# A transformer block on one core: in the lead-in to attention, the placements of the queries go ahead of the swaps on SyncE's queue

## The reference, cut to what matters

```python
# x: (2, 1024, 512); 32 query heads, 8 key/value heads, head size 64
h = _layernorm(x) * (1 + ca) + sa
q = (h @ Wq).reshape(b, s, H, D).transpose(0, 2, 1, 3)
k = (h @ Wk).reshape(b, s, KVH, D).transpose(0, 2, 1, 3)
v = (h @ Wv).reshape(b, s, KVH, D).transpose(0, 2, 1, 3)
q, k = apply_rope(q, pos), apply_rope(k, pos)      # [t1*cos - t2*sin, t1*sin + t2*cos]
scores = einsum('bhqd,bhkd->bhqk', q, repeat(k, 4)) / sqrt(64)
attn = softmax(where(causal, scores, min))
x = x + ga * (einsum('bhqk,bhkd->bhqd', attn, repeat(v, 4)) @ Wo)
h = _layernorm(x) * (1 + cb) + sb
x = x + gb * ffn(h)          # ternary weights, silu gate, rms norm
```

## Time and profile before

| | |
|---|---|
| runs | 1933.04, 1933.71, 1939.78 us; median 1933.71 |
| profiled execution | 1939.95 us, span 1938.1 us, so 1.9 us lie around the span |
| TensorE busy | 1772.3 us, 91% of the span, mean granted clock 0.97 |
| VectorE, ScalarE, GpSimd busy | 1269.1, 1144.7 and 964.6 us |
| attention's first matmul | at 68.7 us |
| first scores of the lead-in | at 111.8 us |
| first transposes of group 0 (L682) | at 127.0 us |

### The profile page before, as it was taken

How to read it: one execution, slowest core, us unless ns; L and a number is a source line. 1 busy time by engine, 2 the same in 40 slices (tenths; PEclk the granted TensorE clock), 3 DMA queues, 4 the chain that set the end, 5 groups by cost and what they waited for, 6 DMA issues and landing times. The chain is left out here.

```text
span 1938.1 us, 28246 instructions
## 1 busy us (share of the span) xinstructions
PE 1772.3 (91%) x9585; PEld 1423.4 (73%) x9585; DVE 1269.1 (65%) x2079; ACT 1144.7 (59%) x2307; POOL 964.6 (50%) x773
## 2 busy tenths in 40 slices
PE   8579999999999999999999999985999599999997
PEld 7367777777777778778777777764888478787876
DVE  6358788778888788788777878783233345444443
ACT  3257777777777877778777777783223243323221
POOL 0127576666666666666765666651000044444443
PEclk8789999999999999999999999997999799999999
DMA  7034353344344343344444433426555200101000
GB/s 258 12 93 114 85 135 108 90 129 110 88 126 109 94 124 101 109 115 108 117 106 102 120 98 91 129 77 225 174 174 176 95 1 1 50 1 50 1 28 22
DMA packets 174922, 190.97 MB, mean 99 GB/s; under 512 B 31408, under 2 KB 117688, under 8 KB 174784
## 3 DMA queue, kind: packets, MB, share of 16 engines
q1 hardware_dynamic: 137792, 140.99, 25.5%
q10 hardware_dynamic: 36992, 48.25, 8.9%
HBM read 86.12 MB, written 31.74 MB: 61 GB/s over the span
## 5 line engine op out<-in xcount | busy, mean ns | idle before, releaser
L814 DVE TENSOR_TENSOR p_lo<-ps_b,p_hi 128x512 fp32r<-128x512 f32 x576 | 395.5, 687 | 193.1 <-ACT p_hi L740 189.0
L753 ACT ACTIVATE p<-ps_b,negm 128x640 f32<-128x640 f32 (+7 forms) x512 | 381.5, 748 | 114.0 <-DVE negm L822 111.3
L740 ACT CAST p_hi<-ps_b 128x512 fp32r<-128x512 f32 x576 | 336.8, 588 | 158.3 <-PE ps_b L682 155.5
L822 DVE TENSOR_REDUCE negm<-ps_b 128x1 f32<-128x640 f32 (+7 forms) x512 | 376.3, 745 | 40.0 <-PE ps_b L674 39.3
L682 PE MATMUL ps_b<-ident,p 128*128 128x128 f32 x2304 | 350.0, 274 | 3.2 <-DVE p_lo L814 2.1
L672 PE MATMUL ps_b<-k_hh,q_hl 128*128 128x512 f32 (+3 forms) x768 | 272.5, 355 | 39.2 <-ACT p L753 36.2
L694 PE MATMUL ps_b<-p_hi,v_hl 128*128 128x512 f32 x576 | 276.7, 480 | 16.3 <-ACT o_sb L746 16.0
L682 PEld LDWEIGHTS ps_b<-ident,p 128*128 128x128 f32 x2304 | 258.7, 141 | 37.3 <-DVE p_lo L814 5.3
L673 PE MATMUL ps_b<-k_l,q_hl 128*128 128x512 f32 (+3 forms) x768 | 258.3, 349 | 0.0
L695 PE MATMUL ps_b<-p_lo,v_hl 128*128 128x512 f32 x576 | 227.7, 395 | 0.0
L672 PEld LDWEIGHTS ps_b<-k_hh,q_hl 128*128 128x128 f32 x768 | 146.5, 191 | 88.4 <-ACT p L753 55.4
(11 more groups left out here) (139 smaller groups left out, 3251.4 us busy)
## 6 DMA issues: line engine op xcount, KB each, us to landing
rot_x<-rot_s SPq DMA_DIRECT2D x320, 64.0 KB, 2.0
q_hl<-rot_s SPq DMA_DIRECT2D x128, 128.0 KB, 2.5
q_hl<-rot_x SPq DMA_DIRECT2D x128, 128.0 KB, 2.5
rd_all<-reciprocals SPq DMA_DIRECT2D x128, 128.0 KB, 3.1
o_low<-o_sb ACTq DMA_DIRECT2D x128, 128.0 KB, 2.4
attention_out<-o_sb SPq DMA_DIRECT2D x128, 128.0 KB, 2.5
o_raw<-attention_out SPq DMA_DIRECT2D x32, 512.0 KB, 4.8
wf<-in_L_ffn_w_gate_up ACTq DMA_DIRECT2D x32, 256.0 KB, 3.1
```

Source lines behind the costliest of these rows:

```text
L740: act.copy(p_hi[:, T % P_RING, :], ps[:, T_BANK + T % 2, :]).then_inc(phi_ready, 1)
L753: act.activation(p_32[:, parity, h, column * P:column * P + nk], s, ACT.Exp, bias=negm[:, k:k + 1], scale=1.0, accum_out=den[:, parity, k: ...
L814: dve.tensor_tensor(p_lo[:, T % P_RING, :], ps[:, T_BANK + T % 2, :], p_hi[:, T % P_RING, :].bitcast(F32), ALU.subtract).then_inc(plo_read ...
L822: dve.tensor_reduce(negm[:, k:k + 1], s, AX.X, ALU.max, negate=True).then_inc(max_ready, 1)
```

## The change

In the lead-in (`body.g < 0`) SyncE issues the placements of a step ahead of its swaps. In the groups (`body.g >= 0`) the order stays.

```diff
             def step(body, T):
-                for g, n, _ in body.uses(T, 5, kinds=("kv", "qx", "qy")):
+                swaps, places = body.uses(T, 5, kinds=("kv", "qx", "qy")), body.uses(T, 10, kinds=("qx", "qy"))
+                if body.g < 0:
+                    for g, n, _ in places:
+                        place(g, n)
+                for g, n, _ in swaps:
                     swap(g, n)
-                for g, n, _ in body.uses(T, 10, kinds=("qx", "qy")):
-                    place(g, n)
+                if body.g >= 0:
+                    for g, n, _ in places:
+                        place(g, n)
```

## The result

| | before | changed |
|---|---|---|
| median of 13 runs, us | 1933.85 | 1940.24 |
| lowest and highest, us | 1932.73, 1939.78 | 1938.05, 1946.60 |
| ratio, 95% interval | | 1.0033 (1.0024 to 1.0043) |
| span of the profiled execution, us | 1938.1 | 1937.9 |

The change costs 6.4 us (4.6 to 8.3), 0.33%. The two profiled spans don't show it: the changed kernel's trace reaches place(9) 1.9 us sooner, loses 4.3 us from there to group 0, and is 2.6 us shorter behind that. Two executions of one kernel differ by several us, and that of before is one of its slower ones. So the traces are compared from a moment that both have in common: the start of place(9), at 98.96 us before and at 97.05 in the changed kernel.

What follows compares the result with a forecast made beforehand. TensorE was taken as the bound (busy 1772 of 1938 us), with group 0's start set by the chain's end. The delay of +4.85 us there, nothing else added, gave 1933.71 + 4.9 = 1938.6 us; range 1934.0 to 1944.5.

Steps and rivals of the forecast that it cites:

- the clock rival: TensorE idles ahead of group 0's first projection and enters it at half clock: +6.5 to +11 us, chance 0.14.
- Step 54: First pair in SyncE's queue: place(9) still begins at 98.96, swap(10) goes from 96.19 to 101.66, 5.5 us later.
- The serial chain with turns of 10.0 us: Swap, sum, low half and placement follow each other: 10.0 us a turn, in place of 8.25 before.
- First scores +1.6: TensorE's first scores, released by place(10)'s landing, start 1.6 us later than 111.75.
- first exponential +3.6 through the table load: On ScalarE the table load follows the later cast of use 11: first exponential at 118.85 in place of 115.22.
- The chain's end sets the start of group 0: Place(12)'s landing releases VectorE's products of use 13, which move 5.9 us; group 0's first projection waits for them, +4.85 us.
- The shift at step 69: Place(12) begins at 128.95 in place of 123.07, +5.9 us, after 2.9 us of slack is used up.
- The prediction's sign for a failed chain: Products of use 13 starting before 131 us would show that the chain isn't serial.
- The seventh row of scores needs the fourth exponential: On TensorE this row waits for ScalarE's fourth exponential: 124.87 becomes about 128.85, +4.0 us.
- The wait of 0.9 us ahead of group 0's first projection: TensorE is there at 133.55 and waits for the products of use 13 until 134.4; against 129.57 that is +4.85 us.
- The faster rival: Low half always ready before the next use's products, so placing first pays: 0 to -2.6 us, chance 0.08.
- Nothing is given back behind the lead-in: From group 0 on all engines carry the delay to the end; the opposing rival, 0 to +3 us, had chance 0.18.

Runs made afterwards that it cites:

- e1: Kernel before with the placement ahead of the swap in step 54 only: median +1.4 us (-0.8 to +3.5) against before.
- e2: Kernel before with placements first in steps 54 and 59, not in step 64: median +4.6 us (+2.7 to +6.6) against before.
- e5: Changed kernel with the exponentials' table loaded early and the cast of use 12 behind the lead-in's last exponential: median +1.5 us (-0.6 to +3.9) against before.
- e9: The changed kernel once more, nothing altered: ratio 1.0038, median +7.3 us (+4.6 to +10.1) against before.
- e3: Changed kernel plus one unused exponential in the lead-in, so the table loads in idle time: median +8.1 us (+5.8 to +10.6) against before.
- e11: Kernel e6 with the cast of use 12 put behind the lead-in's last exponential: median -1.4 us (-3.1 to +0.4) against before.
- e4: Kernel before with the placement ahead of the swap in step 59 only: median -2.5 us (-4.4 to -0.6) against before.
- e6: Kernel e4 with the table of exponentials loaded early: median -3.7 us (-5.8 to -1.7) against before.
- e12: Kernel e6 once more, nothing altered: ratio 0.9994 (0.9983 to 1.0005) against before.

## Why the prediction was right, and where it was wrong

- **The size and the sign.** +4.9 us was forecast, +4.3 measured in the trace and +6.4 (4.6 to 8.3) in the medians; 1940.24 us lies within 1934.0 to 1944.5. By the median alone it could as well be the clock rival, whose stretch began at 1940.2; the trace tells the two apart, with the clock at 1.00 behind the lead-in.
- **Step 54, place(9) gains nothing and swap(10) moves by 5.5 us: right.** Swap(10) was forecast 2.7 us after place(9) and came 2.73 after.
- **The serial chain with turns of 10.0 us: right.** Place(10), (11) and (12) were forecast at +10.0, +20.0 and +30.0 and came at +10.0, +20.0 and +29.8.
- **First scores +1.6, first exponential +3.6 through the table load: right,** with +1.8 and +3.7. e1 against e2 bears that out: with the table load hidden step 54 costs 1.7 us, and with swap(11) late too, so that the load isn't hidden, it is 4.3.
- **"The chain's end sets the start of group 0": wrong.** The text had `await_buffer` of use 13 ask for place(12), and took the meeting of 127.22 us with the landing as its sign. `X_USES` says otherwise: the third column of use 13 is 0, so it shares its buffer with use 11 and asks for place(11), which had long landed. The row's own bracket named TensorE. (The description of the kernel ahead of the prediction has the same mistake.) The shift at step 69, forecast +5.9, is real and measured 5.7, but group 0's start doesn't wait for it (e2, e5). Counted from place(9), the products of use 13 moved by 4.3 us, not 5.9. The prediction's sign for a failed chain was a start before 131. The trace has 129.62, but place(9) is 1.9 us sooner in it: counted from place(9) the sign is at +32.0 and the start at +32.6, so it didn't catch the mistake. The products of use 12 and the chain up to place(12) came as forecast.
- **"The seventh row of scores needs the fourth exponential", +4.0: the size is nearly right, the reason wrong for this execution of the changed kernel.** That row was 3.8 us late, but e2 has the fourth exponential 1.7 us sooner and the row at the same time. TensorE was the one that was late: the fifth row waited for the third exponential and came 3.7 us late, and from there TensorE worked without a pause at its low clock. Where it ran at the higher clock the wait is real: 0.6 us in the repeat e9, 3.76 in e3.
- **The wait of 0.9 us ahead of group 0's first projection: not there.** The delay of the seventh row, 3.8 us, had 0.5 us more added by the low clock, which lasted a little beyond that row here and had ended before it in the kernel before. That gave +4.3 with no wait. The wrong term (4.85) and the right one lie 0.5 us apart by luck.
- **The clock rival.** It did not come in the changed kernel, which had no idle time at that place. It did in e3, where 3.76 us of idle were followed by 6 us at half speed, and group 0 was 2.5 us later than in the changed kernel. The rival asked for an idle time of about 2.6 us; in e11 the clock fell right behind an idle time of 1.96 us.
- **The faster rival** was priced at most 2.6 us, for a case where the placement is ready first. e4 makes that case, and gains 3.7 us in the trace and 2.5 (0.6 to 4.4) in the median. The order of SyncE gave 2.1 us of it, within the price; the 1.6 us on top are the clock between the fifth row and the seventh, a term left out. (In e4 the placement is first in step 59 alone, and step 54 is as before; the rival had looked for its condition in step 54.)
- **Nothing is given back behind the lead-in: not contradicted.** The weight casts keep the shift up to the seventh, the eighth and the end don't, and single traces wander by more than that. The medians speak for it.
- **"The trace disagrees (four issues take longer than one landing)": that comparison shows less than it says.** For a single DMA the same rows give 0.61 us of issue and 2.4 us until it lands. Issue time alone isn't the cause either: of the 5.5 us by which swap(10) moved, 2.8 are the wait for a placement that wasn't ready, and 2.7 its four issues. What the change would cost with cheaper issues no run here shows.

## What to carry to other kernels

Where two transfers meet in one in-order queue, ask pair by pair which is ready first: the order that gains in one step (59) costs in the one before it (54), where a placement that still waits holds a swap that does not. A late transfer costs through what reads it (the first scores, 1.7 us in e1) and through what is queued behind its consumer, so look there too. With a table load moved into idle time and one cast put behind the work it blocked, group 0 started as early as before in the trace (e5), partly by a higher clock. The late cast without the early load was not run. And when a row starts just as some transfer lands, check in the code that it waits for that buffer at all.

## What the runs showed that was not expected

Taking 1.3 us out of ScalarE's path made the start of group 0 later (e3, +6.8 us in the trace against +4.3 without it; the medians, +8.1 and +6.4, have intervals that overlap). TensorE arrived sooner at a wait that did not move, idled 3.76 us, and its granted clock stood at 0.50 for the next 6 us, which were the start of the part that it bounds. The Trainium skill, "TensorE: Matmul & The Clock Gate", Part 1, describes this throttling after idleness; e3's windows agree, with 0.50 from 129 to 135. And the moment at which the clock rises differs between executions of one kernel: within the lead-in, e6 and e12 are 1 us apart for it, the changed kernel and its repeat 0.6 us.
